# Moving the making and transposing of unit rows from the set-up into the first block of a graph-attention kernel, with the masks' first loads re-ordered

## What is computed

```python
cos = beta[0] * (x @ x.T) / (norm2 @ norm2.T + 1e-07)
masked = cos + (1.0 - adj) * -1000000000.0
P = jax.nn.softmax(masked, axis=1)
x = _layernorm(x + P @ x)
x = _layernorm(x + adj @ (x @ weight))
```

## Time and profile before

| | |
|---|---|
| median of 3 runs | 496.63 us |
| profiled execution | 496.09 us, its span 494.3 us |
| TensorE matmul busy | 465.7 us (94%) |
| VectorE busy | 379.5 us (77%) |
| ScalarE busy | 312.8 us (63%) |
| GpSimd busy | 52.5 us (11%) |
| chain that ended last | TensorE 78%, VectorE 9%, DMA 4%, ScalarE 3%, issue 3% |

### The profile page before, as it was taken

The page is one execution under the profiler, slowest core; times in us unless marked ns, Lnnn a source line. Parts: engine busy times, 40 slices in busy tenths (PEclk is TensorE's granted clock), DMA queues, the critical chain, the costliest instruction groups (busy, mean ns, idle before and its releaser), DMA issues.

```text
span 494.3 us, 8871 instructions
## 1 busy us (share of the span) xinstructions
PE 465.7 (94%) x3491; PEld 302.8 (61%) x3491; DVE 379.5 (77%) x637; ACT 312.8 (63%) x358; POOL 52.5 (11%) x64
## 2 busy tenths in 40 slices
PE   0769999999999999999999999999989999999994
PEld 0436676676676676666676766767764455555484
DVE  5979999999999999999999999999973022211253
ACT  4759888898898889889878988987861000000000
POOL 4400000210020020001002002000100000000011
PEclk9989999999999999999999999999999999999998
DMA  7999999999999999998996998970042010011111
GB/s 201 97 110 121 113 114 129 118 148 158 116 146 111 158 146 120 148 139 73 149 141 93 132 136 129 85 148 21 1 172 77 9 39 26 21 44 42 44 42 44
DMA packets 101690, 50.20 MB, mean 102 GB/s; under 512 B 69376, under 2 KB 98208, under 8 KB 101664
## 3 DMA queue, kind: packets, MB, share of 16 engines
q0 software_dynamic: 17952, 16.78, 41.1%
q1 hardware_dynamic: 83424, 33.05, 32.0%
q10 hardware_dynamic: 288, 0.07, 0.1%
HBM read 77.40 MB, written 22.82 MB: 203 GB/s over the span
## 4 chain that ended last, share of the span: by engine, by line
PE 78%; DVE 9%; DMA 4%; ACT 3%; issue 3%; POOL 1%; POOLq 0%; ACTq 0%; DVEq 0%
PE psum L944 22%; PE psum L888 20%; PE psum L892 10%; PE psum L865 9%; PE psum L867 9%; PE psum L866 9%; DVE E L641 4%; ACT E L424 2%; DVE el L649 2%; DMA adjT<-adj_bytes 2%; PE psum L954 1%; DMA adj_bytes<-in_adj 1%; DMA adjT<-in_x 1%; DVE xaug L726 1%; POOL rn L367 1%
## 5 line engine op out<-in xcount | busy, mean ns | idle before, releaser
L888 PE MATMUL psum<-xaug,eh 128*128 128x257 f16 x1024 | 185.9, 275 | 7.8 <-DVE uT L538 4.7
L424 ACT ACTIVATE E<-psum,sc 128x1024 f32<-128x1024 f32 x128 | 154.1, 1204 | 51.7 <-PE psum L867 50.8
L892 PE MATMUL psum<-xaug,el 128*128 128x129 f16 x1024 | 176.7, 222 | 0.0
L641 DVE SCALAR_TENSOR_TENSOR E<-E,adjT 128x1024 f32<-128x1024 f32 x128 | 156.0, 1219 | 14.4 <-ACT E L424 11.8
L649 DVE SCALAR_TENSOR_TENSOR el<-E,eh 128x1024 f16<-128x1024 f32 x128 | 155.8, 1217 | 0.0
L433 ACT ACTIVATE eh<-E 128x1024 f16<-128x1024 f32 x128 | 133.9, 1046 | 1.7 <-DVE E L641 1.7
L888 PEld LDWEIGHTS psum<-xaug,eh 128*128 128x128 f16 x1024 | 99.7, 98 | 36.8 <-DVE uT L538 5.2
L944 PE MATMUL psum<-adjT,uT 128*128 128x512 fp8e4 (+1 forms) x576 | 112.1, 355 | 0.0
L892 PEld LDWEIGHTS psum<-xaug,el 128*128 128x128 f16 x1024 | 100.8, 98 | 13.3
L865 PE MATMUL psum<-uT 128*128 (+1 forms) x256 | 97.9, 382 | 0.0
L866 PE MATMUL psum<-uT 128*128 (+1 forms) x256 | 97.5, 381 | 0.0
(11 more groups left out here) (71 smaller groups left out, 156.7 us busy)
## 6 DMA issues: line engine op xcount, KB each, us to landing
adj_bytes<-in_adj POOLq DMA_DIRECT2D x31, 512.0 KB, 12.4
adjT<-in_x SPq DMA_DIRECT2D x4, 512.0 KB, 6.9
xres<-in_x SPq DMA_DIRECT2D x8, 256.0 KB, 3.5
q_row<-norms SPq DMA_DIRECT2D x8, 256.0 KB, 8.5
x_rows<-x SPq DMA_DIRECT2D x8, 256.0 KB, 2.9
E<-x_rows SPq DMA_DIRECT2D x8, 256.0 KB, 3.0
out<-E SPq DMA_DIRECT2D x16, 128.0 KB, 2.2
x_parts<-x1p SPq DMA_DIRECT2D x7, 256.0 KB, 7.7
```

Of the source, the lines that this page charges most:

```text
L424: nc.scalar.activation(E[:, m % RING, :, :], S[m % 2], ACT.Exp, bias=col(C_BB), scale=col(C_BS)).then_inc(e_done, 1)
L641: nc.vector.scalar_tensor_tensor(out=e, in0=e, scalar=EPRE, in1=mask_bytes(b, m), op0=ALU.mult, op1=ALU.min).then_inc(masked, 1)
L888: return nc.tensor.matmul(O[t][:, 0:XC], eh[:, s, a, cols], xaug[:, j, :], start=start, stop=stop)
L892: return nc.tensor.matmul(O[t][:, 0:D + 1], el[:, s, a, cols], xaug[:, j, 0:D + 1], start=False, stop=False)
```

## The change

- Chunk 0 is squared by VectorE (five rows) and ScalarE (three); of chunks 1 to 3 each takes four (`SQ_V`).
- Unit rows: chunk 0 is made by VectorE as before. Chunk 1 is made by ScalarE ahead of block 0 and chunk 2 by ScalarE behind the exp of pair 4 (`unit_rows_a`: eight activations of one tile each, with a scaled copy of the inverse norms). Chunk 3 is made by VectorE at the end of m = 7.
- Groups: 0 and 1 are turned ahead of block 0, 2 behind the scores of pair 0, 3 behind those of pair 1, all into banks 4 to 7. Groups 4 and 5 are turned ahead of the scores of pair 6, into banks 0 and 1; groups 6 and 7 ahead of those of pair 10, into banks 2 and 3 (`TURN_AT`, `u_bank`). Pairs 6 to 9 use the scores' banks in the opposite order (`bank_of`). The scores of pairs 7 and 11 wait for the low parts of the groups turned just before.
- In block 0 the first weighing is at m = 4 (`LAG0`) and waits for four groups; two weighings stand at the end of block 0.
- xaug is split in five parts (`XPART`), two of them half a chunk, at m = 0, 2, 4, 7, 10.
- The masks' first piece is four parts of one pair. Its first cast is issued when x's first chunk is in, ahead of the first power. The load of the first block's xres stands behind block 0's masks in SyncE's queue.
- The transposed norms go to bank 7 instead of 4.

```diff
@@ -41,7 +41,9 @@
     NC = 4
     CT = NT // NC
     MP = 4
-    FIRST = [(0, 1), (1, 1), (2, 2)]
+    FIRST = [(0, 1), (1, 1), (2, 1), (3, 1)]
+
+    XPART = [(0, 4), (4, 8), (8, 16), (16, 24), (24, 32)]
@@ -222,14 +227,33 @@
         UG = NT // 4
 
         def u_bank(g):
-            return 4 + g % 4
-
-
-        XAUG_AT = (0, 4, 7, 10)
+
+            return 4 + g if g < 4 else g - 4
+
+        XAUG_AT = (0, 2, 4, 7, 10)
+
+        LAG0 = LAG + 1
+
+
+        SQ_V = (5, 4, 4, 4)
 
         def chunk(c):
             return slice(c * CT, (c + 1) * CT)
 
+        def wait_unit_rows(engine, c):
+
+            if c in (1, 2):
+                engine.wait_ge(u_done_a, c)
+            else:
+                engine.wait_ge(u_done, (1, None, None, 2)[c])
+
+
+        TURN_AT = {6: 4, 10: 6}
+
+        def bank_of(m):
+
+            return (m + 1) % 2 if 6 <= m < 10 else m % 2
...
 
 
-        q_turned = psum[0:NT, 4, 0:P]
+        q_turned = psum[0:NT, 7, 0:P]
@@ -247,13 +271,12 @@
             for c in range(NC):
                 half = slice(c * CT // 2, (c + 1) * CT // 2)
                 sp.dma_start(rows_in_twos(xfull)[:, half, :], x_c[:, half, :]).then_inc(x_in[c], 16)
-            sp.dma_start(rows_in_twos(xres[:, :, :]), x_v[0]).then_inc(xres_in, 16)
 
             def load_mask(b, cs=range(MP)):
...
 
             load_mask(0)
+            sp.dma_start(rows_in_twos(xres[:, :, :]), x_v[0]).then_inc(xres_in, 16)
             sp.wait_ge(q_moved, 1)
...
                 b, c = divmod(k, MP)
                 if k == 2:
-                    pool.wait_ge(first_in[k], 16)
+                    pool.wait_ge(first_in[len(FIRST) - 1], 16)
...
+            pool.wait_ge(x_in[0], 16)
+            cast_first(0)
             inverse_norms(0)
-            cast_first(0)
             cast_first(1)
+            cast_first(2)
             inverse_norms(1)
-            cast_first(2)
+            cast_first(3)
             inverse_norms(2)
             inverse_norms(3)
...
-            for c in range(1, NC):
+            for c in range(NC):
                 act.wait_ge(x_in[c], 16)
-                for t in range(c * CT + CT // 2, (c + 1) * CT):
+                for t in range(c * CT + SQ_V[c], (c + 1) * CT):
                     last = nc.scalar.activation(work[:, t, :], xfull[:, t, :], ACT.Square, accum_out=n2[:, t:t + 1])
                 last.then_inc(squares_a, 1)
@@ -408,7 +434,19 @@
                 act.wait_ge(uT_filled, g + 1)
                 nc.scalar.activation(uT_out(0, g), uT_in(g), ACT.Copy).then_inc(uT_hi, 1)
 
+            def unit_rows_a(c):
+                act.wait_ge(rn_done, c + 1)
+                if c > 1:
+                    act.wait_ge(u_done_a, c - 1)
+                nc.scalar.activation(rn_a[:, :], rn[:, chunk(c)], ACT.Copy, scale=USC).then_inc(rn_scaled, 1)
+                act.wait_ge(rn_scaled, c)
+                for t in range(CT):
+                    last = nc.scalar.activation(work[:, c * CT + t, :], xfull[:, c * CT + t, :], ACT.Copy,
+                                                scale=rn_a[:, t:t + 1])
+                last.then_inc(u_done_a, 1)
+
@@ -421,7 +459,7 @@
                 act.wait_ge(scaled, (n + 1) * small + 1)
                 if later(b) or m >= RING:
                     act.wait_ge(lo_done, n - RING + 1)
-                nc.scalar.activation(E[:, m % RING, :, :], S[m % 2], ACT.Exp,
+                nc.scalar.activation(E[:, m % RING, :, :], S[m % 2 if later(b) else bank_of(m)], ACT.Exp,
                                      bias=col(C_BB), scale=col(C_BS)).then_inc(e_done, 1)
@@ -434,9 +472,9 @@
                                      scale=ECAST).then_inc(hi_done, 1)
 
             def xaug_hi(c):
+                ts = slice(*XPART[c])
                 act.wait_ge(xs_step, 5)
-                nc.scalar.activation(xaug[:, chunk(c), 0:D], xfull[:, chunk(c), :], ACT.Copy,
-                                     scale=col(C_XS)).then_inc(x_hi, 1)
+                nc.scalar.activation(xaug[:, ts, 0:D], xfull[:, ts, :], ACT.Copy, scale=col(C_XS)).then_inc(x_hi, 1)
...
             for m in range(NP):
+                if m in TURN_AT:
+                    uT_hi_part(TURN_AT[m])
+                    uT_hi_part(TURN_AT[m] + 1)
                 exp_pair(0, m)
+                if m < 2:
+                    uT_hi_part(m + 2)
+                if m == 4:
+                    unit_rows_a(2)
                 if m in XAUG_AT:
                     xaug_hi(XAUG_AT.index(m))
-                if m == 1:
-                    split_hi(0, 0)
-                if m < LAG:
-                    uT_hi_part(2 * m + 2)
-                    uT_hi_part(2 * m + 3)
-                if m > 1:
+                if m > 0:
                     split_hi(0, m - 1)
...
             def sum_squares(c):
                 dve.wait_ge(x_in[c], 16)
-                for t in range(c * CT, c * CT + (CT if c == 0 else CT // 2)):
+                for t in range(c * CT, c * CT + SQ_V[c]):
...
             def clamp(c):
                 dve.wait_ge(squares_v, c + 1)
-                if c > 0:
-                    dve.wait_ge(squares_a, c)
+                dve.wait_ge(squares_a, c + 1)
...
             sum_squares(0)
             clamp(0)
             sum_squares(1)
-            sum_squares(2)
             clamp(1)
             unit_rows(0)
+            sum_squares(2)
+            clamp(2)
             sum_squares(3)
-            clamp(2)
             clamp(3)
             partition_extremes()
             uT_lo_part(0)
             extremes()
-            unit_rows(1)
             scales()
             uT_lo_part(1)
             dve.wait_ge(rn_done, NC)
             nc.vector.reciprocal(q[:, :], rn[:, :]).then_inc(norms, 1)
-            unit_rows(2)
             small = dve.value_load(flag[0:1, 0:1], min_val=0, max_val=1)
-            unit_rows(3)
...
-                if not later(b) and m < 3:
+                if not later(b) and m < len(FIRST):
@@ -722,10 +758,10 @@
                 nc.vector.tensor_tensor(dst[:, :, 1, :], x1[:, :, :], dst[:, :, 0, :], ALU.subtract).then_inc(x1_split, 1)
 
             def xaug_lo(c):
+                ts = slice(*XPART[c])
                 dve.wait_ge(x_hi, c + 1)
-                nc.vector.scalar_tensor_tensor(out=xaug[:, chunk(c), D + 1:XC], in0=xfull[:, chunk(c), :],
-                                               scalar=col(C_XS), in1=xaug[:, chunk(c), 0:D], op0=ALU.mult,
-                                               op1=ALU.subtract).then_inc(x_lo, 1)
+                nc.vector.scalar_tensor_tensor(out=xaug[:, ts, D + 1:XC], in0=xfull[:, ts, :], scalar=col(C_XS),
+                                               in1=xaug[:, ts, 0:D], op0=ALU.mult, op1=ALU.subtract).then_inc(x_lo, 1)
...
-                    if m == 1:
-                        split_lo(0, 0)
-                    if m < LAG:
-                        uT_lo_part(2 * m + 2)
-                        uT_lo_part(2 * m + 3)
+                    if m == 0:
+                        uT_lo_part(2)
                     if m in XAUG_AT:
                         xaug_lo(XAUG_AT.index(m))
-                    if m > 1:
+                    if m == 1:
+                        uT_lo_part(3)
+                    if m > 0:
                         split_lo(0, m - 1)
+                    if m + 1 in TURN_AT:
+                        uT_lo_part(TURN_AT[m + 1])
+                        uT_lo_part(TURN_AT[m + 1] + 1)
+                    if m == 7:
+                        unit_rows(3)
...
             def turn_unit_rows(g):
-                pe.wait_ge(u_done, g * 4 // CT + 1)
-                if g > 3:
-                    pe.wait_ge(uT_lo, g - 3)
+                wait_unit_rows(pe, g * 4 // CT)
...
-                    o = S[m % 2][:, a, :]
+                    o = S[m % 2 if later(b) else bank_of(m)][:, a, :]
...
+            def weigh_first(m):
+                for c, (t, _) in enumerate(XPART):
+                    if t == 2 * m:
+                        pe.wait_ge(x_lo, c + 1)
+                weigh(m, m)
+
             for m in range(NP):
-
-                if m // 2 < UG:
-                    pe.wait_ge(uT_lo, m // 2 + 1)
+                if m in TURN_AT:
+
+                    pe.wait_ge(e_done, m - 1)
+                    turn_unit_rows(TURN_AT[m])
+                    turn_unit_rows(TURN_AT[m] + 1)
+
+                    pe.wait_ge(e_done, m)
+
+                pe.wait_ge(uT_lo, m // 2 + 1)
+                if m - 1 in TURN_AT:
+                    pe.wait_ge(uT_lo, TURN_AT[m - 1] + 2)
                 if m == 1:
                     pe.wait_ge(maxima, 1)
                 scores(0, m)
+                if m == 0:
+                    turn_unit_rows(2)
                 if m == 1:
                     pe.wait_ge(norms, 1)
                     nc.tensor.transpose(q_turned, q[:, :], ident[:, :]).then_inc(q_filled, 1)
                     pe.wait_ge(q_moved, 1)
-                if m < LAG:
-                    turn_unit_rows(2 * m + 2)
```

(25 more changed lines are left out.)

## The result

The changed kernel takes 501.49 us (median, 500.54 to 502.28), the kernel before, timed beside it, 495.98. The ratio is 1.0099 (interval 1.008 to 1.0118): it is slower by 1%. By the ratio that is 4.9 us (4.0 to 5.9), by the difference of the two medians, of four executions each, 5.5. The profiled execution took 501.44 us, 5.35 more than that of before, and its span is 5.3 longer.

The account below looks back on a forecast made before the run. Before, TensorE sets the pace; after the change the load of pairs 4 to 7 holds mask 4 and uT behind it. 496.1 + 3.1 for block 1 opening later + 1.5 for the clock = 500.7 us, range 495.0 to 503.2.

Parts of the forecast that it names:

- scores 7 to scores 11, with the clock: Block 0: 12.8 us of VectorE work until scores 11 may start, plus 1.5 us for the clock's fall.
- scores 11 to block 1: TensorE, end of block 0: five scores and six weighings, 6.5 + 8.0 = 14.5 us.
- block 1 opens: Block 1's first scores on TensorE: at 68.8 to 70.3, instead of 65.73 before.
- It lands at 34.3: Transposed load of pairs 4 to 7: lands at 34.3, against 35.2 before; ends 31.5 to 36.7.
- mask 4 then waits for its load until 34.4: VectorE, block 0: the mask of pair 4 is held by its load until 34.4, not by ScalarE's exp.
- The late load's rival (36.7): Load of pairs 4 to 7 shares DMA engines with an earlier second cast, landing at 36.7: 503.1 us, chance 0.15.
- The 7.1 us from mask 4 to scores 7: VectorE's queue from mask 4 through the low parts of groups 4 and 5: 7.1 us, so scores 7 at 41.5.
- This cost lies beside the load's wait: ScalarE's work, including chunk 2's unit rows, ends at 37.3 to 38.2, before VectorE gets to uT at 40.2.
- One fall was forecast: TensorE's clock falls after the idle time before scores 7, as before, costing 1.5 us; other end none.
- the forecast 4.3 us: TensorE idle from the end of weighing 2, about 37.2, to scores 7 at 41.5: 4.3 us.
- The rival in which the first load is early: Load of pairs 4 to 7 lands by about 32.5 and the clock holds: 495.0 to 498.6 us, chance 0.30.
- The faster rival (493.5): Shorter set-up, ScalarE alone decides: first exp at 16.0, scores 7 at 35.8, load in by 28.5; 493.5 us, chance 0.12.

Follow-up runs that it names:

- experiment 6: Changed kernel with masks of pairs 4 to 15 of block 0 using the bytes of pairs 0 to 3, waiting for no load: 496.6 us, ratio 1.0008.
- experiment 8: Changed kernel with the piece of pairs 4 to 7 cast and loaded in two halves: 496.51 us, ratio 1.0009.
- Experiment 2: Changed kernel with high parts of groups 4 and 5 right behind exp 5, low parts right behind mask 4: 499.41 us, ratio 1.0046.
- experiment 3: Changed kernel with seven of ScalarE's eight activations for chunk 2's unit rows left out: 501.53 us, ratio 1.0099.
- experiment 4: Changed kernel with the old order of loads (first piece in three parts, first cast behind the first power, xres first): 499.58 us, ratio 1.0062.
- experiment 7: Changed kernel with TensorE kept busy around pair 6 by extra matmuls and by turning group 5 three times: 500.47 us, ratio 1.0082.
- experiment 1: Changed kernel with masks of pairs 4 to 7 of block 0 using the bytes of pairs 0 to 3, without their load wait: 499.43 us, ratio 1.0045.
- experiment 5: Kernel before with only the new order of the loads: 496.45 us, ratio 0.9996.
- experiment 9: Changed kernel with pairs 4 to 7 in halves, groups 6 and 7 turned ahead of scores 8, chunk 3's rows at m = 4: 497.09 us, ratio 1.0011.
- experiment 10: Changed kernel with halves, groups 6 and 7 turned ahead of scores 8, and ScalarE making chunk 2's rows ahead of the first exp: 497.49 us, ratio 1.0011.
- experiment 11: Changed kernel with halves and ScalarE making chunk 2's rows ahead of the first exp, without the earlier turns: 496.64 us, ratio 1.0002.

## Why the prediction was right

The forecast was 500.7 us; 501.49 was measured, with the mechanism that it names. By its steps, forecast against the profile of the change:

| step | forecast | measured |
|---|---|---|
| cast of pairs 4 to 7 issued | 16.5 | 16.18 |
| the cast lands | 26.6 | 26.8 |
| its load lands | 34.3 | 34.6 |
| mask 4 starts, held by the load | 34.4 | 34.64 |
| scores 6 | 34.5 | 33.92 |
| weighing 2 ends | 37.2 | 38.4 |
| scores 7 | 41.5 | 41.81 |
| scores 7 to scores 11, with the clock | 12.8 + 1.5 | 14.75 |
| scores 11 to block 1 | 14.5 | 14.52 |
| block 1 opens | 70.3 | 71.08 |
| profiled execution | 500.7 | 501.44 |

The close figure owes something to luck: the cast took 10.6 us, not 10.1, and was issued 0.3 us sooner than summed, and a fall of the clock that the sum left out is covered by the wait. The forecast of the whole change was 4.6 us, in the profiles it is 5.35.

**The load.** "It lands at 34.3" and "mask 4 then waits for its load until 34.4" hold within 0.3 us. Experiments 6 and 8 show the cause: with the masks' bytes there, or with only the load of pairs 4 to 7 divided, which also brings in that of pairs 8 to 11 sooner, the whole loss is gone. The late load's rival (36.7) did not come about: the next cast was issued at 27.54, 0.8 behind the start of the load, and the load took 7.8 us.

**The queue behind it.** The 7.1 us from mask 4 to scores 7 were 7.17. Experiment 2 shows that this part of the sum is real: without it 2.1 us come back.

**ScalarE.** "This cost lies beside the load's wait" holds, by experiment 3. The eight activations of chunk 2 took 2.44 us, from 28.10 to 30.70 with the scaled copy ahead of them: 2.6, the low end of the 2.6 to 3.4 that was taken.

**The clock.** One fall was forecast, of 1.5 us, after the wait before scores 7. There were two. The first, at 33.9, was not foreseen: I had asked only what the long wait does, not the two short ones ahead of it. It made scores 6 and weighing 2 take 4.5 us instead of 2.6 and cost nothing itself, being covered by the load's wait; it shortened the idle time before scores 7 from the forecast 4.3 us to 3.4, and the clock fell again all the same. The second fall cost 1.3 us by the traces of experiments 4 and 7, not 1.5. Without it scores 7 to 11 took 13.45 us, not 12.8: mask 7 waits 0.7 us for the exp of scores 7, which the sum had only with the clock.

**What the prediction lacked.** It treats the load of pairs 4 to 7 as the only late one. Experiments 1 and 5 show the next: pairs 8 to 11 land at 47 to 49, and would have been the bound as soon as the first was not. It also says that VectorE waited only for pair 2's load in the kernel before; an earlier mask, at 20.23, waited 0.39 us for its load as well, which changes nothing here. The rival in which the first load is early had 495.0 to 498.6, and holds only where the second is early too: with the first load alone out of the way experiment 1 measured 499.43 in the median, though four of its ten executions took under 498; with both out of the way it was 496.6, and with both brought forward, 496.5. The faster rival (493.5) has no support: even with all loads there the time is that of before; in experiment 8 the first half was in by 26.4, inside the 28.5 that this rival asked for, and the time was 496.5.

**Where the expected gain went.** The first weighing did come 6 us sooner. In experiment 6, with no load in the way of pairs 4 to 15, ScalarE's rows between exp 4 and exp 5 hold scores 6 until 33.67, and the clock falls there. Scores 7 still start 3.7 us sooner than before (37.97 against 41.71). But behind them stand one weighing more (1.3 us), two more groups to turn (0.9) and the wait of 1.88 us before scores 11, and the lead is gone. Experiments 9 to 11 moved the waits about without removing them. In experiments 10 and 11 VectorE was busy without a pause from the first mask until the low parts that scores 7 wait for were done. Whether an order exists that keeps the lead remains open; the change makes chunk 3's unit rows on VectorE in block 0, and no version takes work off VectorE there.

## What to carry to other kernels

Before work is moved into a stretch, look at what stands there that is hidden now, loads above all, and ask when it lands against when it will be wanted: here a load 0.6 us earlier than before became the bound, because its user came 5 us earlier. In an in-order queue, place what another engine waits for ahead of an instruction that can be held by a load; behind it, the wait is the load's plus all that lies between. And divide the load whose first part is wanted first: that alone returned the whole 5 us here, while in the kernel before, where this load was not what mask 4 waited for, a gain isn't shown. Behind the limit that is removed look for the next: here they were a load, the next load, ScalarE's rows, and VectorE's own work.

## What the runs showed of the hardware

TensorE's clock fell to 0.50, the 1.2 GHz level, after two waits of 1.82 and 1.92 us with eight transposes between them, and again in one of 3.40. After a single wait of 1.89 (experiment 3, before scores 6) or 1.88 (experiment 6, before scores 11) it stayed at 1.00, and in experiment 4, after one of 1.32, it did not fall again. With filler matmuls in the waits it stayed at 1.00 throughout. The Trainium skill ("TensorE: Matmul & The Clock Gate", Part 1: The HAM clock gate, What's actually happening) says that the throttled state is the default and that activity releases it; the run with filler matmuls agrees. Filling the waits made the median 1.0 us lower, although the waits themselves were for other engines.

A transposed load of four pairs took 7.8 and 10.2 us beside a cast and 5.0 where the next cast was issued only 1.4 us before its end (the change's loads issued at 26.8, 38.5 and 45.4). Dividing cast and load brought mask 4 forward by 4.9 us, from 34.64 to 29.76, and the load of pairs 8 to 11 in by 44.8 instead of 48.7, at no cost elsewhere that the runs show.
